# A written table of slots for the loop's tasks, and the gate's narrow products in turn with two runs of values

## The chip, the cores and the metric

One core of one Trainium2 chip runs the whole kernel as one launch. The metric is the device time in microseconds (us) of that launch; for the kernel before, three runs are shown and their median is the number that counts. Four compute engines matter here: TensorE (PE in the profile; its weight loads are PEld), VectorE (DVE), ScalarE (ACT) and GpSimd (POOL). SyncE (SP) only issues DMAs.

## The reference

One layer over 1024 tokens of width 256, in float32: a layer norm, then an attention and a mixture of experts on the same normed rows, both added to the input.

```python
q, k, v = heads(xn @ Wq.T), heads(xn @ Wk.T), heads(xn @ Wv.T)      # 16 heads of 16
scores = einsum('bhid,bhjd->bhij', q, k) / sqrt(16)
std_out = out_proj(softmax(where(mask, scores, neg)))
...
gsa_scores = scores + position_sensitivity * splat_attn              # 8 splats a head
gsa_out = out_proj(softmax(where(mask, gsa_scores, neg)))
attn = (1 - blend) * std_out + blend * gsa_out

logits = xn @ gate_w.T                                               # 16 experts
scores = sqrt(softplus(logits));  top 2 of scores + gate_b
out = einsum('eci,edi->ecd', silu(buf @ W1) * (buf @ W3), W2)        # 128 slots an expert
y = weighted sum of the two experts' rows + shared expert
return x + attn + y
```

So there are two softmaxes for each of the 16 heads over a causal 1024 x 1024 matrix, and beside them 16 routed experts of 128 slots and one shared expert for all 1024 tokens.

## The kernel before

**Prologue.** TensorE's tasks are listed in `PRO`: transposes of the normed rows (`xnT`), projections of the first half of q and k (`proj`), the splats' parameters (`par`), splat features of the first half (`feat`), the gate's logits (`gate`, L736), the values (`v`, four runs, L751), then the second half's projections (`proj1`, L702). Task n of the list goes to PSUM bank n % 5 and waits until the task five before it has been emptied. The gate is 16 products of 128 x 128 weights with 16 columns, each two float32 instructions (32 on the trace); one `v` run is 4 products of 256 columns (8 instructions). The first two `v` runs stand right behind the gate; then TensorE takes the first maxima of group 0 (L770, L775), with the last two `v` runs between them. These maxima need q and k, which SP brings into `stage` (L348).

**Loop.** Eight groups of two heads (g = 0 to 7); in each, six pairs of key blocks (p = 0 to 5), and in each pair four turns, so 24 slots a group. A pair does on TensorE: `pv` of the pair before (L897, 16 instructions), slot 0, `splat` for s = 0 (L879), slot 1, `splat` for s = 1, slot 2, `std` of the next pair for s = 0 (L867, and L870 on the diagonal), slot 3, `std` for s = 1. ScalarE does one exponential (L670) a turn, and then what the slot has for it. VectorE has no work of the attention's own but the copies of the accumulator: `evac` (L1281) before slot 0 (of the group before) and before slot 8. TensorE's first `pv` of the next accumulation waits for that copy.

**Slots.** `PLAN[g][n]` lists the tasks of slot n. Each engine walks the same list in order and takes its own share:
- `max`, `max2` (TensorE L775, L770; VectorE L1215, L1183): row maxima for the next group's softmax shift, 14 tasks a group. In group 0 eight more `pre` maxima of group 0 itself. The last of each half leads to a chain of small VectorE operations, and `shift` (L778, L1229) turns the result; SP then writes it into `qs` (L369).
- `xT`, `gu`, `hT`, `y` of an expert (L801, L813, L817, L822), `sgu`, `shT`, `sy` of a part of the shared one; `weights` and `y` let SP load weights (L520, L521). GpSimd gathers an expert's rows (L452).
- `route` 0 to 7, `rest`, `third`, `product`, `add`: VectorE only (but for two products of `route`); `square`, `p0`, `p1`: ScalarE only; `feat1`: four feature products of the second half (L712) with a ScalarE evacuation (L588).
- `oT`, `oTh`, `rows`, `out`: the output side (L826, L830, L839, L852).

Tasks that need PSUM share three banks (5 to 7) in the order of the table: the task three before has to be emptied first. So TensorE, which runs strictly in order, stops at such a task when VectorE or ScalarE is behind.

**How the slots are given.** Helpers place families of tasks: `spread_late` puts maxima on slots that are no multiple of 4, two a slot; `chain` repeats an expert's steps every 12 slots; `spread` and the list `HALF` place the rest. They are the same for groups 1 to 6.

Of the kernel before, what the change touches and what calls it, by code (L numbers as in the profile page):

```python
# [6 lines left out]
def bass_splat_attention_moe_layer(nc, x, wqkvo, params, w13, w2, ws13, ws2, out):  # L7
# [3 lines left out]
    T, D = x.shape  # L11
# [32 lines left out]
    with ctx:  # L44
# [147 lines left out]
        PRO += [("feat", (tc, w)) for tc in range(NC) for w in range(2)] + [("gate", 0)] + [("v", n) for n in range(NT // 2)]  # L192
# [38 lines left out]
        def slotted(*lists):  # L231
            slots = [[] for _ in range(NSLOT)]
            for entries in lists:
                for at, t in entries:
                    slots[at].append(t)
            return slots

        ROUTE = 8
        CUM, IDS = 4, 7

        def spread_late(tasks, first, last):
            late_slots = [n for n in range(first, last + 1) if n % 4]
            return [(late_slots[len(late_slots) * n // len(tasks)], t) for n, t in enumerate(tasks)]

        def spread(tasks, first, last):
            return [(first + (last + 1 - first) * n // len(tasks), t) for n, t in enumerate(tasks)]

        def chain(steps, count, at, period):  # L250

            return [(at + period * (n // 2) + slot, (kind, n)) for n in range(count) for kind, slot in steps[n % 2]]
        SHARED = ((("sgu", 2), ("shT", 5), ("sy", 6)), (("sgu", 7), ("shT", 9), ("sy", 10)))
        EXPERT = ((("xT", 0), ("gu", 2), ("hT", 5), ("y", 6)), (("xT", 5), ("gu", 7), ("hT", 9), ("y", 10)))

        maxima = spread_late(max0, 0, 6) + [(9, ("shift", 0))] + spread_late(max1, 7, 20) + [(22, ("shift", 1))]
        LATER = 8
        first_rest = [(n // 2, ("pre", t)) for n, t in enumerate(max1[LATER:])] + [(4, ("pre", ("shift", 1)))]
        first_maxima = spread_late(max0, 5, 9) + [(12, ("shift", 0))] + spread_late(max1, 10, 20) + [(22, ("shift", 1))]

        HALF = [(2, ("square", 0)), (3, ("square", 1)),
                (4, ("feat1", (0, 1))), (5, ("feat1", (1, 1))), (6, ("feat1", (0, 0))), (7, ("feat1", (1, 0))),
                (8, ("p0", 4)), (9, ("p0", 5)), (24, ("rest", 4)), (26, ("rest", 5)), (28, ("p1", 4)), (30, ("p1", 5)),
                (34, ("third", 4)), (37, ("third", 5)), (42, ("product", 1)), (44, ("p0", 6)), (46, ("p0", 7)),
                (48, ("rest", 6)), (50, ("rest", 7)), (52, ("p1", 6)), (55, ("p1", 7)), (58, ("third", 6)), (62, ("third", 7))]
        LAST_FEAT = ("feat1", (1, 0))
        S_ROUTE, S_SHARED, S_EXPERT, S_ADD = (8, 31), (32, 148), 56, 156
        OWN_AT = (0, 3)  # L270
        long = HALF + spread([("route", k) for k in range(ROUTE)], *S_ROUTE)

        for half in range(2):
            long += [(at, (kind, n + half * NT // 2)) for at, (kind, n) in chain(SHARED, NT // 2, S_SHARED[half], 12)]
        long += [(S_EXPERT - 24 + 5 * e, ("weights", e)) for e in range(WB - 1)]
        long += chain(EXPERT, E, S_EXPERT, 12)
        long += spread([("add", (k, n)) for n in range(NT) for k in range(2)], S_ADD, 7 * NSLOT + 16)
        AT = {t: at for at, t in long}
        PLAN = []
        for g in range(NG):  # L280
            lists = [[(11, ("oT", 0))], [(at - g * NSLOT, t) for at, t in long if at // NSLOT == g]]
            if g:
                lists.append([(3, ("oT", 1))])
            else:
                lists.append(first_rest)
            if g < NG - 1:
                lists.append(maxima if g else first_maxima)
            if g == NG // 2:
                lists.append([(14, ("rows", (0, 0))), (18, ("rows", (0, 1)))])
            if g == NG - 1:  # L290
                lists.append([(6, ("out", (TC, 0))), (10, ("out", (TC + 2, 0))), (13, ("rows", (1, 0))),
                              (16, ("out", (0, 2))), (19, ("out", (2, 2))), (21, ("oTh", 0))])
            PLAN.append(slotted(*lists))

# [401 lines left out]
        def _(pe):  # L696
# [18 lines left out]
            def prologue(n):  # L715
# [15 lines left out]
                elif kind == "gate":  # L731
                    pe.wait_ge(par_in, 16)
                    pe.wait_ge(pro_act, KD * NC)
                    for t in range(NT):
                        for k in range(KD):
                            last = M(b[:, t * E:(t + 1) * E], xnT[:, k, t * P:(t + 1) * P], gw_sb[:, k, :],  # L736
                                     start=k == 0, stop=k == KD - 1)
# [9 lines left out]
                else:  # L747
                    pe.wait_ge(wvo_in, 32)
                    for i in range(2):
                        for k in range(KD):  # L750
                            last = M(b[:, i * D:(i + 1) * D], xnT[:, k, (2 * a + i) * P:(2 * a + i + 1) * P],  # L751
                                     wt[:, 2, k, :], start=k == 0, stop=k == KD - 1)
# [657 lines left out]
```

## Time and profile before

| | us |
|---|---|
| median of three runs | 357.77 |
| lowest, highest | 357.11, 359.34 |
| the profiled execution, its own time | 356.44 |
| its span, first to last instruction | 354.7 |

| engine | busy us of the span | share |
|---|---|---|
| TensorE | 316.1 | 89% |
| VectorE | 235.8 | 66% |
| ScalarE | 201.4 | 57% |
| GpSimd | 39.7 | 11% |

The span leaves 1.7 us of the execution's time outside. The loop's first `std` starts at 52.2 us and the loop's last `pv` at 345.7 us. TensorE's matmuls are pipelined, so a busy TensorE in a row of the profile can hide short stalls; the granted clock is 1.00 for 2.4 GHz and 0.50 for 1.2 GHz.

### The profile page before, as it was taken

The numbers are of one execution on the slowest core, as the hardware profiler recorded it, in microseconds if no ns is written. First come the engines' busy times: TensorE is split into PE (matmuls) and PEld (weight loads), VectorE is DVE, ScalarE is ACT, GpSimd is POOL, SyncE is SP. The second block draws the span as 40 slices with busy tenths as digits, with TensorE's granted clock in tenths as the row PEclk, the third lists the DMA queues.
The fourth block names the chain that finished last, engine by engine and source line by source line (L and its number), as shares of the span: only waits on it lengthen the run. The fifth ranks groups of instructions, "written<-read, shape, count | busy, mean of one in ns | idle before, by whom it ended". The sixth has DMA issues, their size and how long they took to land.

```text
span 354.7 us, 6091 instructions
## 1 busy us (share of the span) xinstructions
PE 316.1 (89%) x2064; PEld 161.2 (45%) x2064; DVE 235.8 (66%) x735; ACT 201.4 (57%) x300; POOL 39.7 (11%) x59
## 2 busy tenths in 40 slices
PE   0899898977779999999999999999999999999984
PEld 0548533223423455444544455445445554445352
DVE  4858776499997568964766567665766568666424
ACT  1696277575645576654565465555555545647730
POOL 7300000000020000111111111102110004444000
PEclk9998998999978999999999999999999999999999
DMA  7424353224146303635455536554554443222011
GB/s 243 132 43 65 57 99 88 55 43 67 30 65 167 73 2 48 137 112 138 112 140 116 161 87 146 129 143 100 128 145 134 102 80 78 59 72 60 7 59 59
DMA packets 25790, 33.54 MB, mean 95 GB/s; under 512 B 4636, under 2 KB 18556, under 8 KB 25756
## 3 DMA queue, kind: packets, MB, share of 16 engines
q1 hardware_dynamic: 24056, 28.85, 35.3%
q0 software_dynamic: 1536, 4.20, 4.3%
q8 instruction: 18, 0.29, 0.3%
q14 instruction: 16, 0.13, 0.1%
q10 hardware_dynamic: 164, 0.07, 0.1%
HBM read 16.15 MB, written 4.26 MB: 58 GB/s over the span
## 4 chain that ended last, share of the span: by engine, by line
PE 44%; DVE 5%; ACT 2%; issue 2%; DMA 1%; SPq 1%; DVEq 0%
PE ps L897 12%; PE ps L813 6%; PE ps L822 5%; PE ps L879 5%; PE ps L867 4%; PE ps L775 4%; PE ps L852 2%; DMA stage<-split 1%; PE ps L817 1%; PE ps L870 1%; ACT arena_p L670 1%; DVE mx L1215 1%; ACT small L682 1%; PE ps L826 1%; PE ps L801 1%
## 5 line engine op out<-in xcount | busy, mean ns | idle before, releaser
L670 ACT ACTIVATE arena_p<-ps 128x1024 f32<-128x1024 f32 (+1 forms) x192 | 148.0, 808 | 49.6 <-PE ps L879 29.2
L897 PE MATMUL ps<-arena_p,v_full 128*32 128x512 f32 (+3 forms) x768 | 72.6, 496 | 0.0
L1183 DVE CUSTOM_DVE_ANT_0 ps<-ps,mask_r 128x128 f32<-128x128 f32 (+3 forms) x128 | 61.7, 501 | 11.6 <-PE ps L775 6.9
L775 PE MATMUL ps<-stage 96*128 96x512 bf16 (+3 forms) x160 | 50.6, 354 | 8.1 <-DVE mx L1215 3.7
L867 PE MATMUL ps<-stage 98*128 98x512 bf16 (+1 forms) x192 | 51.6, 333 | 3.7 <-ACT arena_p L670 3.0
L1215 DVE TENSOR_REDUCE mx<-ps 128x1 f32<-128x512 f32 x64 | 43.9, 686 | 14.5 <-PE ps L775 14.1
L879 PE MATMUL ps<-stage 98*128 98x512 bf16 (+1 forms) x192 | 47.2, 334 | 2.5 <-ACT arena_p L670 2.3
L452 POOL DMA_INDIRECT wt<-xn_scratch,ids_sb x16 | 15.3, 954 | 235.3 <-PE ps L801 107.6
L897 PEld LDWEIGHTS ps<-arena_p,v_full 128*32 128x32 f32 x768 | 20.1, 110 | 34.6 <-issue 30.0
L775 PEld LDWEIGHTS ps<-stage 96*128 96x128 bf16 x160 | 15.6, 99 | 29.6 <-issue 22.2
L675 ACT ACTIVATE small<-ps 128x176 f32<-128x176 f32 x24 | 7.6, 317 | 37.2 <-PE ps L813 37.2
L879 PEld LDWEIGHTS ps<-stage 98*128 98x128 bf16 x192 | 15.6, 99 | 28.8 <-ACT arena_p L670 13.1
L867 PEld LDWEIGHTS ps<-stage 98*128 98x128 bf16 x192 | 18.6, 99 | 19.5 <-ACT arena_p L670 5.8
L1237 DVE SCALAR_TENSOR_TENSOR small<-small,ps 128x176 f32<-128x176 f32 x24 | 8.1, 338 | 29.0 <-ACT small L675 12.7
L822 PE MATMUL ps<-arena_o,small 88*128 88x256 f32 x96 | 25.7, 389 | 1.9 <-ACT small L682 1.8
L870 PE MATMUL ps<-mask_t,ident_b 128*128 128x128 bf16 x128 | 25.9, 221 | 0.0
L682 ACT ACTIVATE small<-ps 88x256 f32<-88x256 f32 x24 | 9.1, 379 | 29.3 <-PE ps L817 28.0
L813 PE MATMUL ps<-w_sb,wt 128*128 128x352 f32 x64 | 22.3, 471 | 1.2 <-DVE wt L1231 0.9
L822 PEld LDWEIGHTS ps<-arena_o,small 88*128 88x128 f32 x96 | 16.9, 189 | 8.3 <-issue 5.5
L477 POOL DMA_INDIRECT split<-ye_scratch,gidx x16 | 15.4, 962 | 45.9 <-DMA ye_scratch<-wt 28.8
L1005 DVE TENSOR_TENSOR acc<-ps,acc 128x256 f32<-128x256 f32 (+1 forms) x14 | 7.5, 538 | 16.2 <-PE ps L852 11.3
L1183 DVE DVE_READ_ACCUMULATOR2_ANT mx<- 128x1 f32 x128 | 18.1, 142 | 0.0
(199 smaller groups left out, 374.2 us busy)
## 6 DMA issues: line engine op xcount, KB each, us to landing
w_sb<-in_w_dram SPq DMA_DIRECT2D x16, 352.0 KB
stage<-split SPq DMA_DIRECT2D x48, 96.0 KB
stage<-split SPq DMA_DIRECT2D x96, 32.0 KB
stage<-split SPq DMA_DIRECT2D x48, 64.0 KB
arena_o<-in_w_dram SPq DMA_DIRECT2D x16, 176.0 KB
ye_scratch<-wt SPq DMA_DIRECT2D x16, 128.0 KB, 2.6
stage<-split SPq DMA_DIRECT2D x32, 48.0 KB
acc<-in_x_dram SPq DMA_DIRECT2D x2, 512.0 KB, 4.7
```

Of the source, the lines that this page charges most:

```text
L452: nc.gpsimd.indirect_dma_start(out=xe[:, e % XB, :], out_offset=None, in_=xn_d[:, :], in_offset=bass.IndirectOffsetOnAxis(ap=ids_sb[:, e:e ...
L477: nc.gpsimd.indirect_dma_start(out=gath[:, k, n, :], out_offset=None, in_=ye_d[:, :], in_offset=bass.IndirectOffsetOnAxis(ap=gidx[:, k, n: ...
L670: A(to, ps[:, 1 + 2 * s:3 + 2 * s, off:CH], ACT.Exp, scale=SCALE).then_inc(done, 1)
L775: ins = M(b[:, 0:n1 - n0], qs[0:KR, pr, h, it * P:(it + 1) * P], ks[0:KR, pr, h, n0:n1], start=True, stop=True)
L813: ins = M(b[:, 0:2 * I], lhs, w13_sb[:, wb, k, :], start=k == 0, stop=k == KD - 1)
L822: ins = M(b[:, 0:D], hT[:, c, :], w2_sb[:, wb, c, :], start=c == 0, stop=c == 1)
L867: ins = M(b[:, off:CH], ks[:, pr, h, (jb + s) * P:(jb + s + 1) * P], qs[:, pr, h, ic * CH + off:(ic + 1) * CH], start=True, stop=not diag)
L870: ins = M(b[:, off:off + P], ident_b[:, :], mask_t[:, :], start=False, stop=True)
L879: ins = M(ps[:, 1 + 2 * s + h, off:CH], fk[:, pr, h, (jb + s) * P:(jb + s + 1) * P], fq[:, pr, h, ic * CH + off:(ic + 1) * CH], start=Fals ...
L897: ins = M(ps[c:c + 2 * HD, 0, off:CH], v_full[:, jb + s, g * GH + h, :], of, start=jb + s == 0, stop=end or last, skip_group_check=last an ...
L1183: return V.tensor_tensor_reduce(row, row, mask_r[:, CH - row.shape[1]:CH], 1.0, NEG, ALU.add, ALU.max, to)
L1215: V.reduce_max(to, b[:, 0:n1 - n0], AX.X).then_inc(aux_free, 1)
```

## The change

Two edits.

**The table.** The helpers and lists that made `PLAN` are gone, and all 8 x 24 slots are written out. Same tasks, same three banks, same engines; what differs is the slot, and the order within a slot. `AT` is read back from the table. The task that starts SP's load of the shared weights, the loads of q, k and features and so on still hang on the same tasks and slots.

**The prologue.** `("v", 0)` now stands before `("gate", 0)` in `PRO`, and the three tasks `v 0`, `gate`, `v 1` are issued by one function: two tokens' blocks of the gate (8 instructions), one block of values (4 instructions), four times over. It waits at its start for all three banks, for the values' weights, for the parameters and for all of `xnT`.

```diff
-        PRO += [("feat", (tc, w)) for tc in range(NC) for w in range(2)] + [("gate", 0)] + [("v", n) for n in range(NT // 2)]
+        PRO += [("feat", (tc, w)) for tc in range(NC) for w in range(2)] + [("v", 0), ("gate", 0), ("v", 1), ("v", 2), ("v", 3)]
...
-        maxima = spread_late(max0, 0, 6) + [(9, ("shift", 0))] + spread_late(max1, 7, 20) + [(22, ("shift", 1))]
...
+        PLAN = [
+            [
+                [("pre", ("max", (1, 4, 0))), ("pre", ("max", (1, 4, 1))), ("pre", ("max", (1, 5, 0))),
+                 ("pre", ("max", (1, 5, 1)))],
+                [("pre", ("max", (1, 6, 0))), ("pre", ("max", (1, 6, 1))), ("pre", ("max", (1, 7, 0)))],
+                [("pre", ("max", (1, 7, 1)))],
+                [("max2", (0,))],
+                [("square", 0), ("square", 1), ("pre", ("shift", 1))],
+                [("max2", (1,)), ("p0", 4), ("max", (0, 2, 0))],
+                [("feat1", (0, 1)), ("feat1", (1, 1)), ("max", (0, 3, 0))],
+                [("max", (1, 2, 0))],
+                [("max", (1, 3, 0)), ("route", 0)],
+                [("p0", 5)],
+                [("max", (0, 4, 0)), ("feat1", (0, 0)), ("feat1", (1, 0)), ("max", (0, 4, 1)), ("max", (0, 5, 0)),
+                 ("max", (0, 5, 1))],
+                [("route", 1), ("oT", 0)],
+                [("shift", 0), ("max", (0, 6, 0))],
+                [("max", (0, 6, 1)), ("max", (0, 7, 0)), ("max", (0, 7, 1)), ("max", (1, 4, 0))],
+                [("max", (1, 4, 1)), ("route", 2), ("route", 3)],
...
+                [("route", 5), ("rest", 5)],
+            ],
...
-                elif kind == "gate":
-                    pe.wait_ge(par_in, 16)
-                    pe.wait_ge(pro_act, KD * NC)
-                    for t in range(NT):
-                        for k in range(KD):
-                            last = M(b[:, t * E:(t + 1) * E], xnT[:, k, t * P:(t + 1) * P], gw_sb[:, k, :],
-                                     start=k == 0, stop=k == KD - 1)
...
+            def gate_and_values():
+
+                n = PRO.index(("gate", 0))
+                for at in (n - 1, n, n + 1):
+                    pe.wait_ge(*emptied[at - PB])
+                pe.wait_ge(wvo_in, 32)
+                pe.wait_ge(par_in, 16)
+                pe.wait_ge(pro_act, KD * NC)
+                gates, runs = ps[:, n % PB, :], (ps[:, (n - 1) % PB, :], ps[:, (n + 1) % PB, :])
+                for half in range(NT // 2):
+                    for t in (2 * half, 2 * half + 1):
                         for k in range(KD):
...
+                            scores = M(gates[:, t * E:(t + 1) * E], xnT[:, k, t * P:(t + 1) * P], gw_sb[:, k, :],
+                                       start=k == 0, stop=k == KD - 1)
+                    if half == NT // 2 - 1:
+                        scores.then_inc(pro_full, 1)
+                    last = values(half, half % 2, runs[half // 2])
+                    if half % 2:
+                        last.then_inc(pro_full, 1)
```

The slots that the prediction speaks of, before and after (read from both tables; "3:5" is slot 5 of group 3; `m h it pc` is a `max` of head h, row block it, key half pc):

| task | before | after |
|---|---|---|
| `pre` maxima of group 0 | 2 in each of 0:0 to 0:3 | 4 in 0:0, 3 in 0:1, 1 in 0:2 |
| `square` 0, 1 | 0:2, 0:3 | both 0:4 |
| `feat1` (0,1), (1,1) | 0:4, 0:5 | both 0:6 |
| `feat1` (0,0), (1,0) | 0:6, 0:7 | both 0:10 |
| `max2` 0 and 1 of group 0 | 0:5, 0:5 | 0:3, 0:5 |
| `p0` 4, 5 | 0:8, 0:9 | 0:5, 0:9 |
| `m 1 3 0`, `route` 0 | 0:9, 0:8 | 0:8, 0:8 |
| `route` 1, 2, 3 | 0:11, 0:14, 0:17 | 0:11, 0:14, 0:14 |
| `rest` 4, 5 | 1:0, 1:2 | 0:19, 0:23 |
| `route` 5, 6, 7 | 0:23, 1:2, 1:5 | 0:23, 1:1, 1:6 |
| `max2` 0, 1 in group 3 | both 3:1 | 3:2, 3:3 |
| `hT` 3, `y` 3 | 3:5, 3:6 | 3:4, 3:6 |
| `shift` 0, `xT` 4, `gu` 4 | 3:9, 3:8, 3:10 | 3:8, 3:9, 3:11 |
| `m 0 6 1`, `m 0 7 0`, `m 0 7 1` | 3:11, 3:11, 3:13 | 3:11, 3:12, 3:12 |
| `xT` 6, `gu` 6 | 3:20, 3:22 | 3:18, 3:22 |
| maxima in 6:5 | 1 (and 1 in 6:6, 2 in 6:7) | 5 (none in 6:6, 6:7) |
| `out` (0,2), (2,2) | 7:16, 7:19 | 7:18, 7:19 |
| `oTh` 0 | 7:21 | 7:23 |

No slot before has more than two maxima. After, ten slots have three or more (0:0, 0:1, 0:10, 0:13, 0:17, 1:18, 5:1, 5:9, 6:5, 6:10). `hT`, `y` and `xT` of the other experts stay or move by one or two slots.

## Rows read from the trace of the kernel before

**Rows 1.** The page: span, and busy time of each engine.
```profile
span 354.7 us, 6091 instructions
PE 316.1 (89%) x2064; PEld 161.2 (45%) x2064; DVE 235.8 (66%) x735; ACT 201.4 (57%) x300; POOL 39.7 (11%) x59
```

**Rows 2.** Busy by stretch: length, PE, PEld, DVE, ACT, POOL, granted clock, DMA, GB/s.
```profile
27.44:30.97 3.53, 3.53 (x34) 3.53 (x32) 3.20 (x4) 2.97 (x4) 0.00 (x0) 1.00 0.33 57
30.97:34.38 3.41, 3.41 (x10) 2.78 (x11) 3.31 (x3) 1.93 (x2) 0.00 (x0) 0.50 0.60 84
...
52.17:54.86 2.69, 1.65 (x12) 0.85 (x13) 0.95 (x3) 2.68 (x4) 0.00 (x0) 1.00 0.87 190
54.86:58.28 3.42, 3.42 (x13) 1.64 (x12) 2.17 (x5) 3.12 (x5) 0.00 (x0) 0.50 0.36 82
58.28:69.21 10.93, 10.69 (x63) 3.25 (x61) 4.87 (x21) 5.21 (x10) 0.00 (x0) 1.00 0.22 35
69.21:102.65 33.44, 25.37 (x215) 10.68 (x214) 30.99 (x107) 21.64 (x27) 0.00 (x0) 1.00 0.29 52
102.65:105.93 3.28, 2.75 (x7) 0.92 (x7) 3.11 (x14) 1.41 (x2) 1.84 (x2) 0.50 0.52 78
105.93:109.48 3.55, 3.55 (x23) 1.24 (x23) 1.42 (x5) 2.05 (x2) 0.21 (x1) 0.50 0.73 218
...
175.25:211.55 36.30, 34.91 (x245) 18.28 (x243) 23.04 (x76) 20.41 (x33) 3.78 (x4) 1.00 0.52 134
...
321.72:354.70 32.98, 26.47 (x190) 13.19 (x188) 14.44 (x36) 14.15 (x20) 2.81 (x3) 1.00 0.15 48
```

**Rows 3.** Who TensorE waited for, 69.3 to 106 us: total, times, longest.
```profile
PE ps L775 <- DVE mx L1215: 2.0, 2, 1.7
...
PE ps L784 <- DVE mx L1183: 1.8, 1, 1.8
...
PE ps L826 <- DVE mx L1183: 1.0, 1, 1.0
```

**Rows 4.** Timeline of TensorE in the prologue: start, length, instructions, idle before.
```profile
27.44 3.82 PE L736 MATMUL ps<-prm,xx 128*128 128x16 f32 x32
31.10 5.31 PE L751 MATMUL ps<-wt,xx 128*128 128x256 f32 x16
36.25 0.50 PE L770 MATMUL ps<-stage 96*128 96x128 bf16 x4
...
36.75 1.89 PE L751 MATMUL ps<-wt,xx 128*128 128x256 f32 x8
38.48 0.54 PE L775 MATMUL ps<-stage 96*128 96x512 bf16 x2
...
42.52 0.22 PE L778 MATMUL ps<-ident_b,mhl 128*16 128x128 bf16 x1 [1.55 <-DVE mhl L1005]
```

**Rows 5.** Timeline of SyncE's queue, 18 to 42 us: the loads of q and k.
```profile
19.68 11.72 SPq L348 DMA_DIRECT2D stage<-split  x12
```

**Rows 6.** The page's DMA issues: count, KB each, us from issue to landing.
```profile
ye_scratch<-wt SPq DMA_DIRECT2D x16, 128.0 KB, 2.6
```

**Rows 7.** Who VectorE waited for, 52 to 58.9 us.
```profile
DVE mx L1215 <- PE ps L775: 4.3, 3, 2.7
```

**Rows 8.** Who VectorE waited for, 58.9 to 69.3 us.
```profile
DVE ps L1183 <- PE ps L775: 3.3, 2, 2.0
```

**Rows 9.** Timeline of TensorE: a feature product of two steps, and what follows.
```profile
63.85 1.08 PE L712 MATMUL ps<-xx,small 128*64 128x512 f32 x4 [0.24 <-ACT rest L588]
...
65.72 0.34 PE L775 MATMUL ps<-stage 96*128 96x384 bf16 x1
```

**Rows 10.** Timeline of VectorE: the first and the last end of route 0.
```profile
70.74 0.28 DVE L1005 TENSOR_TENSOR g_last<-w_sb,prm 128x128 f32<-128x128 f32 x1
...
72.68 0.70 DVE L1183 CUSTOM_DVE_ANT_0 ps<-ps,mask_r 128x512 f32<-128x512 f32 x1
```

**Rows 11.** Who TensorE waited for in group 3, 175.25 to 211.55 us (six such rows).
```profile
PE ps L822 <- ACT small L682: 0.3, 1, 0.3
```

More of the change, by code:

```diff
@@ L229, in bass_splat_attention_moe_layer @@
         max1 = [("max", (h, it, pc)) for h in range(GH) for it in range(TC, NT) for pc in range(2)]
[L231 to L236, printed above, removed]
         ROUTE = 8
         CUM, IDS = 4, 7
-        def spread_late(tasks, first, last):
-            late_slots = [n for n in range(first, last + 1) if n % 4]
-            return [(late_slots[len(late_slots) * n // len(tasks)], t) for n, t in enumerate(tasks)]
@@ L247, in spread @@
[L247 to L254, printed above, removed]
@@ L256, in bass_splat_attention_moe_layer @@
-        maxima = spread_late(max0, 0, 6) + [(9, ("shift", 0))] + spread_late(max1, 7, 20) + [(22, ("shift", 1))]
-        LATER = 8
[L258 to L267, printed above, removed]
+        LATER = 8
@@ L268, in bass_splat_attention_moe_layer @@
         LAST_FEAT = ("feat1", (1, 0))
-        S_ROUTE, S_SHARED, S_EXPERT, S_ADD = (8, 31), (32, 148), 56, 156
         OWN_AT = (0, 3)
[L271 to L277, printed above, removed]
@@ L295, in bass_splat_attention_moe_layer @@
+        AT = {t: g * NSLOT + n for g, slots in enumerate(PLAN) for n, tasks in enumerate(slots) for t in tasks
+              if t[0] not in ("max2", "max", "shift", "pre", "oT")}
         END = [("rowsh", 0), ("oTh", 1), ("out", (TC, 1)), ("rowsh", 1), ("out", (TC + 2, 1))]
@@ L749, in prologue, with values @@
                     for i in range(2):
-                        for k in range(KD):
-                            last = M(b[:, i * D:(i + 1) * D], xnT[:, k, (2 * a + i) * P:(2 * a + i + 1) * P],
-                                     wt[:, 2, k, :], start=k == 0, stop=k == KD - 1)
-                last.then_inc(pro_full, 1)
+                        last = values(2 * a + i, i, b)
+                last.then_inc(pro_full, 1)
+            def values(t, i, b):
+                for k in range(KD):
+                    last = M(b[:, i * D:(i + 1) * D], xnT[:, k, t * P:(t + 1) * P], wt[:, 2, k, :], start=k == 0, stop=k == KD - 1)
+                return last
+            def gate_and_values():
[8 more added lines that the diff above has]
+                    for t in (2 * half, 2 * half + 1):
+                        for k in range(KD):
+                            scores = M(gates[:, t * E:(t + 1) * E], xnT[:, k, t * P:(t + 1) * P], gw_sb[:, k, :],
[4 more added lines that the diff above has]
+                    if half % 2:
+                        last.then_inc(pro_full, 1)
             def weights_of(kind, a):
@@ L929, in _ @@
             n_v, n_p = PRO.index(("v", 0)), PRO.index(("proj1", (0, 0)))
-            for n in range(n_v + 2):
+            for n in range(n_v):
                 prologue(n)
+            gate_and_values()
             pe.wait_ge(wide_ready, 1)
@@ L941, in _ @@
                 if n in (AB, 2 * AB - 1):
-                    prologue(n_v + 2 + n // 4)
+                    prologue(n_v + 3 + n // 4)
                 aux(-1, t, 0)
```

208 lines of the change are left out of this document (192 added, 16 removed).

## The prediction

> **What bounds the kernel now.** I read the page first: TensorE is busy 316.1 of 354.7 us [rows 1]. That says "TensorE", and for most of the loop it is right, but a share of the span hides where it is not. So I cut the span into stretches [rows 2]. In a steady group (the fourth, 36.30 us) TensorE is busy 34.91 us, so 1.39 us is all that a better order can take off there, save for drains too short for the profile. VectorE has 23.04 us of work in it. The stretch 69.21 to 105.93 us (most of group 0 and the start of group 1) is another matter: VectorE is busy 30.99 + 3.11 = 34.10 of 36.72 us, TensorE only 25.37 + 2.75 = 28.12, so TensorE idles 8.60 us. The waits name the cause: TensorE stood 2.0 + 1.8 + 1.0 us for VectorE's maxima to empty a bank [rows 3]; the routing runs on VectorE between them. VectorE bounds this stretch. And right ahead of it, 52.17 to 69.21 us, VectorE is busy only 0.95 + 2.17 + 4.87 = 7.99 of 17.04 us: the engine that bounds the next 37 us had idled for 9.05.
>
> The third thing is the granted clock. It is 1.00 nearly everywhere and 0.50 in three stretches [rows 2]: 30.97 to 34.38, 54.86 to 58.28, and 102.65 to 109.48 us. Before the second and third TensorE had gaps; before the first it had none (busy 3.53 of 3.53 us), but all it did was the gate's narrow products.
>
> **The change, part by part.**
>
> *Gate and values.* The 32 narrow instructions took 31.10 - 27.44 = 3.66 us at clock 1.00; the 16 instructions of two value runs behind them took 36.25 - 31.10 = 5.15 us, mostly at 0.50; at 1.00, eight take 38.48 - 36.75 = 1.73 us, so sixteen 3.46 [rows 4]. Same instructions after the change, so at full clock the block takes 3.66 + 3.46 = 7.12 us where it took 8.81: 1.69 us less, if the clock holds. It should: no long run of narrow products is left, each eight (0.9 us) is followed by 0.87 us of 256-column ones. Does the gain travel on? Next is the first maximum, which needs q and k. SP issued the last of these loads at 19.68 + 11.72 = 31.40 us [rows 5]; with the 2.6 us that a larger transfer takes to land [rows 6] that is 34.0, about when TensorE would now come (34.6). VectorE had finished its splitting work about then too, and idled until the first maximum. What comes next, up to the loop's first `std`, is a chain through TensorE and VectorE (1.55 us wait at 42.52 us, [rows 4]) and shifts as a whole. The block's new wait at its start is for three banks at once, those of the second parameter task and of the first two features, which VectorE and ScalarE empty before the last features that TensorE computes ahead of the block; the gate's reader (VectorE, behind the first maxima) comes long after the block. I take -1.6, with bounds 0 (clock falls all the same, or q and k late) and -1.7.
>
> The Trainium skill ("TensorE: Matmul & The Clock Gate", section "HAM oscillation — how this bites in real kernels") lays a fallen clock to gaps in which TensorE idles. By that rule the interleaving would bring nothing here, since the block has no gap before or after; the sum would be 1.6 us smaller. The row at 27.44 us, no idle and a fall at its end, speaks against the rule being all there is, and I go by the row; what it would mean is a rival below.
>
> *Groups 0 and 1.* VectorE's work is conserved, so the end of its bound stretch moves by as much of its earlier idling as the table removes. Two places. First, slot 0:0 now has four maxima, 0:1 three: of the three waits for a maximum (4.3 us, longest 2.7) the longest stands before the loop's first product and stays, the other 1.6 go, less about 0.2 [rows 7]. Second, the features. A product of two steps takes TensorE 65.72 - 63.85 = 1.87 us [rows 9], two of them 3.7 us, in which VectorE gets nothing: it waited 3.3 us for two maxima behind these [rows 8]. Now both stand in 0:10, where VectorE has in hand `m 1 3 0` and `m 0 4 0` (0.6 each, a 512-column one takes 0.70) and `route` 0 (72.68 - 70.74 = 1.94 us) [rows 10]: 3.2 of the 3.7 us are covered. Together 1.4 + 3.2 = 4.6 us. TensorE can follow, as it idles 8.60 us in the stretch. Against it: `square` 0 and 1 both in 0:4 hold ScalarE for two microseconds ahead of an exponential, but `pv` covers most of it; `rest` 4, 5 (1.2 us each) now stand before the group's end, ahead of `evac`, so the first `pv` of group 1 waits for VectorE, where before the waits stood a little later. It is the same debt, paid elsewhere. SP: the shared weights' load hangs on the last feature, now 0:10; the feature loads of slots 0:7 and 0:8 no longer queue behind it, the q and k loads of 0:10 on still do; their readers come 20 us later. I take -4.6, bounds 0 and -8.6.
>
> *The loop's clock.* The low stretches of the loop, 3.42 and 6.83 us long, cost at most half: 1.7 and 3.4 us. Where gaps will fall next I can't say; the worst TensorE waits shrink, but a new one stands at the end of group 0. I take 0, bounds -3.4 and +3.4.
>
> *Steady groups 2 to 5.* Six waits of 0.2 to 0.3 us a group, such as `y` on ScalarE's copy [rows 11]. `hT` 3 is a slot further from `y` 3, `xT` 6 four slots ahead of `gu` 6 instead of two, `max2` no longer right behind `hT` and `xT`, `m 0 7 0` not right behind `gu` and `oT`. That aims at all six. Some come back in other places, so I take 0.6 of 1.39 us, four times: -2.4. Bounds: -5.6, and +2.8 if one 512-column maximum (0.70 us, [rows 10]) a group is waited for anew. SP's order is nearly that of before: `y` moves by a slot at most, and the last q and k loads are needed a slot later in group 3. The gathers on GpSimd have an expert's step to spare.
>
> *Groups 6 and 7.* Five maxima in 6:5 with three banks: VectorE frees one every 0.6 us, so TensorE waits about 1 us there, and saves the small waits behind; 0. In the last stretch TensorE idles 6.5 of 32.98 us [rows 2], mostly in the dependent ending. The output products now stand after both `splat`s of their pair and `oTh` after the last, so that ScalarE's exponential and VectorE's copy are covered: -0.4, bounds -1 and +1.
>
> Sum: -1.6 - 4.6 + 0 - 2.4 + 0 - 0.4 = -9.0 us. The profiled execution took 356.44 us (span 354.7), so 347.4; the median of the runs shown is 1.33 above it, so 348.8.
>
> **Rivals.** About 1% (3.6 us) is what a measurement of this kernel can tell from no change.
>
> (a) The clock falls in the prologue all the same, or was never the narrow products' doing: all but the first term, 350.4. For it, the rule above; against it, the row. 0.12.
>
> (b) The lead of VectorE is lost at the seam of groups 0 and 1: `route` 5, `rest` 5, `evac` and `route` 6 stand in one row on VectorE, over 7 us, and TensorE behind them waits so long that it pays 3 us of idling and 1.7 us of low clock. Then 353.5. For it: TensorE would reach group 1 well ahead of VectorE. Against: the debt stands before, too. 0.13.
>
> (c) Slower: the bunches. Ten slots have three or more maxima on three banks; the old table spread them two by two. Each maximum past the banks costs TensorE 0.6 us if VectorE is not idle when the bunch comes, and it is busy 23.04 of 36.30 us even in a steady group. At 1.5 us a bunch that is +15, against -9: 364. The point from which it decides is 1.3 us a bunch (+12.6, past +1%). Against it: slots behind a bunch are left empty, and in group 0 VectorE wants the work. 0.08.
>
> (d) The stalls only move: TensorE is the bound at 89% and its work is unchanged, gains of 2 us or less, 356. 0.07.
>
> The forecast itself, 344.5 to 352.5, has 0.60.
>
> **How the numbers follow.** Faster by over 1% (under 354.2): 0.60 + 0.12 + most of (b), 0.08: 0.80. Same: the rest of (b), and (d): 0.12. Slower: (c), 0.08. The range from 344.0 to 355.5 takes in (a) and (b) and leaves (c), (d) and a larger gain (the clock's -3.4) out: about 0.2.
>
> **What would show it.** Prologue: the rows of the block (L736 and L751 now mixed) in 7.1 us, and granted clock 1.00 from 27 to 37 us; the loop's first L867 at 50.5 instead of 52.17. Group 0: VectorE idle between first L867 and the 9th us of features down from 9.05 to about 4.5 us; the L897 run that opened at 105.93 (second of group 1) at about 99 to 100. Steady groups 35.7 us instead of 36.30. The forecast is wrong if that L897 run stands after 103, if a steady group grows, or if waits of TensorE on L1215 or L1183 behind the bunches sum to over 5 us.

## The result and the profile after

| | before | after |
|---|---|---|
| median of the runs measured side by side | 358.29 us (4 runs) | 342.33 us (4 runs) |
| range of these runs | 357.11 to 359.34 | 340.96 to 344.22 |
| profiled execution | 356.44 us | 344.22 us |
| its span | 354.7 us | 342.4 us |

The changed kernel is faster: ratio 0.956, 95% interval 0.950 to 0.962, some 16 us. The forecast was 348.8 us with a range down to 344.0, so the sign was right and the size wrong, beyond the lower end. The two profiles are 12.2 us apart; the profile of after happens to be the slowest of its four executions, that of before is below its median, and the 3.7 us between the two differences are taken up further down.

The page of the kernel after, its span and its engines, to be held against [rows 1]:

```profile
span 342.4 us, 6091 instructions
PE 309.8 (90%) x2064; PEld 159.4 (47%) x2064; DVE 236.4 (69%) x735; ACT 201.1 (59%) x300; POOL 39.6 (12%) x59
```

The instructions are the same in number. PE's busy time is 6.3 us lower, since some of it was time at the lower clock and some was waiting that its records don't show as such; the other 6.0 us of the shorter span are idle time that is gone. Busy time by stretch of the kernel after (length, PE, PEld, DVE, ACT, POOL, granted clock, DMA, GB/s), for [rows 2]: the block of gate and values; two stretches from the loop's first `std` to the second `pv` of group 1; groups 2 to 6 whole.

```profile
29.11:36.25 7.14, 7.14 (x51) 6.63 (x50) 6.51 (x6) 5.38 (x6) 0.00 (x0) 1.00 0.46 69
52.16:68.68 16.52, 14.66 (x98) 5.71 (x100) 11.21 (x41) 14.34 (x19) 0.00 (x0) 1.00 0.42 81
68.68:101.01 32.33, 26.88 (x209) 11.25 (x205) 29.89 (x104) 19.65 (x26) 0.65 (x1) 0.96 0.33 55
...
132.09:166.44 34.35, 34.11 (x244) 17.99 (x242) 25.12 (x75) 21.82 (x34) 3.78 (x4) 1.00 0.48 117
166.44:201.43 34.99, 34.73 (x245) 18.22 (x244) 23.70 (x79) 20.47 (x33) 3.78 (x4) 1.00 0.57 139
201.43:236.39 34.96, 34.83 (x251) 18.99 (x249) 25.31 (x80) 19.89 (x32) 3.78 (x4) 1.00 0.57 142
236.39:272.70 36.31, 35.05 (x244) 17.98 (x242) 22.14 (x72) 20.86 (x34) 1.89 (x2) 1.00 0.49 124
272.70:310.46 37.76, 35.38 (x238) 17.47 (x236) 23.08 (x70) 20.48 (x34) 13.23 (x14) 1.00 0.29 71
```

The block is 7.14 us long at clock 1.00, where it was 8.81. In groups 2 to 4 PE idles 0.24, 0.26 and 0.13 us; before, group 3 alone had 1.39 [rows 2]. The only wait of TensorE left in group 3 (engine, tile, line, whom it waited for: us in total, times, longest) stands where there were six [rows 11]:

```profile
PE ps L1042 <- ACT arena_p L829: 0.2, 1, 0.2
```

Here is the whole difference between the two profiles. The marks are the starts of instructions in the timelines; a group runs from its first `pv` to that of the next group.

| stretch | before | after | difference | forecast |
|---|---|---|---|---|
| start to the block of gate and values | 27.44 | 29.11 | +1.67 | none |
| the block, to the first maximum | 8.81 | 7.14 | -1.67 | -1.6 |
| to the loop's first `std` | 15.92 | 15.91 | 0.0 | 0 |
| to the start of group 2 | 86.08 | 79.93 | -6.15 | -4.6 |
| groups 2 to 5 | 147.56 | 140.61 | -6.95 | -2.4 |
| group 6 | 35.91 | 37.75 | +1.84 | 0 |
| group 7, to its last `pv` | 24.00 | 22.89 | -1.11 | -0.4 (with the ending) |
| ending | 8.98 | 9.10 | +0.1 | |
| sum | 354.70 | 342.44 | -12.2 | -9.0 |

### The profile page after: what moved, and what is told of

The parts are those of the page before. It is cut to its first block, busy times and chain, and to the rows that moved or that the text cites. A ratio compares the mean times of both kernels' runs of the same rounds, so it can differ in the third digit from the quotient of the medians.

```text
span 342.4 us, 6091 instructions
## 1 busy us (share of the span) xinstructions
PE 309.8 (90%) x2064; PEld 159.4 (47%) x2064; DVE 236.4 (69%) x735; ACT 201.1 (59%) x300; POOL 39.6 (12%) x59
## 4 chain that ended last, share of the span: by engine, by line
PE 73%; SPq 9%; DVE 9%; ACT 4%; issue 2%; DMA 2%; DVEq 0%
PE ps L1072 19%; PE ps L1042 9%; PE ps L988 9%; PE ps L1054 8%; PE ps L997 7%; PE ps L950 7%; SPq L507 4%; SPq L522 3%; PE ps L861 2%; PE ps L1027 2%; ACT arena_p L829 2%; PE ps L1001 2%; SPq L519 2%; DVE ps L1359 2%; PE ps L871 2%
## 5 line engine op out<-in xcount | busy, mean ns | idle before, releaser
L1042 PE MATMUL ps<-stage 98*128 98x512 bf16 (+1 forms) x192 | 50.9, 330 | 5.7 <-ACT arena_p L829 3.4
L950 PE MATMUL ps<-stage 96*128 96x512 bf16 (+3 forms) x160 | 49.3, 344 | 5.8 <-DVE mx L1359 3.5
L1054 PE MATMUL ps<-stage 98*128 98x512 bf16 (+1 forms) x192 | 45.4, 326 | 0.1
L1457 DVE COPY pv_sb<-ps 128x512 f32<-128x512 f32 x15 | 10.4, 691 | 10.0 <-PE ps L1072 9.9
```

The lines of the kernel that those rows point to most:

```text
L950: ins = M(b[:, 0:n1 - n0], qs[0:KR, pr, h, it * P:(it + 1) * P], ks[0:KR, pr, h, n0:n1], start=True, stop=True)
L1042: ins = M(b[:, off:CH], ks[:, pr, h, (jb + s) * P:(jb + s + 1) * P], qs[:, pr, h, ic * CH + off:(ic + 1) * CH], start=True, stop=not diag)
L1054: ins = M(ps[:, 1 + 2 * s + h, off:CH], fk[:, pr, h, (jb + s) * P:(jb + s + 1) * P], fq[:, pr, h, ic * CH + off:(ic + 1) * CH], start=Fals ...
```

## The experiments

The new table writes out every group, so each part of the change can be put into the old kernel, or taken out of the new one, alone. "Old slots" are those that the expressions removed by the diff give, written out as a table. All ratios are to the kernel before, measured on the same chip in turn with it. "Low" is a stretch at granted clock 0.50. A task is written as in the prediction; `m` is a maximum.

### The prologue alone, the table alone

**e1_prologue**: old slots, new order of gate and values.

```
-  PRO += [...] + [("gate", 0)] + [("v", n) for n in range(NT // 2)]
+  PRO += [...] + [("v", 0), ("gate", 0), ("v", 1), ("v", 2), ("v", 3)]
```

> The prologue's edit alone, on the table of before. Theory A (narrow products brought the clock down): the block of gate and values takes 7.1 us at granted clock 1.00 instead of 8.8 us, and the first maximum follows at once; 1.7 us faster than before in a profile with an equal start, ratio about 0.995, no other stage changed. Rival (the fall belongs to the moment, not to the products): a low stretch still falls on or right behind the block in the profile, and the ratio is 1.000.

Measured: ratio 0.996 (0.992 to 1.000; 10 runs against 11), so that the total alone can't be told from no change; the stage shows it. In its profile the block is 7.13 us long at clock 1.00, and the first `std` comes 23.04 us after the block's start, where it came 24.73 after: 1.69 us less, the forecast's number. The groups are as before (38.66, 40.67, 37.21, 36.30, 37.95, 36.30, 35.92, 24.00). The block in the busy time by stretch:

```profile
28.55:35.68 7.13, 7.13 (x51) 6.63 (x50) 6.50 (x6) 5.38 (x6) 0.00 (x0) 1.00 0.45 69
```

**e2_table**: new table, old prologue (the diff's `PRO` line undone).

> The written table alone, on the prologue of before. Theory: it carries nearly all, about 12 to 14 of the 16 us between the medians, ratio 0.960 to 0.966; the block of gate and values keeps its 8.8 us with clock 0.50 behind the narrow products. Rival (the two edits need each other, the earlier start of the maxima being what feeds VectorE): ratio 0.975 or more.

Measured: ratio 0.960 (0.953 to 0.967). Block 8.81 us, low from 30.6 to 34.0. So nearly all of the gain is the table's, 14.4 us between the medians (342.97 against 357.35). From the first `std` to the second `pv` of group 1 (the distance that the prediction speaks of: 53.76 us before) it takes 46.76, to group 2 77.77 where before took 86.08.

### Which groups

**e3_groups01**: before, with the new slots in groups 0 and 1. **e4_groups2345**: before, with the new slots in groups 2 to 5.

```
-  PLAN = [ <old slots of groups 0 to 7> ]
+  PLAN = [ <new slots of groups 0, 1>, <old slots of groups 2 to 7> ]      # e3
+  PLAN = [ <old slots of groups 0, 1>, <new of 2 to 5>, <old of 6, 7> ]    # e4
```

> The new slots of groups 0 and 1 only; groups 2 to 7 and the prologue as before. Theory (VectorE's early idling is filled): from the loop's first std to the second pv of group 1, 48.8 us instead of 53.8, and about 6 us off up to the start of group 2's second pair; groups 2 to 5 stay at 36.3 to 38.0 us each. Ratio 0.980 to 0.985. Rival (the lead of the first groups is what shortened groups 2 to 5 too, by loads and gathers that come earlier): groups 2 to 5 shorten by 1 us or more each, ratio under 0.975.

Measured: ratio 0.974 (0.967 to 0.981), profile 348.49 us. The place is right and the size larger than expected. The second `pv` of group 1 stands 46.77 us after the first `std`, as with the whole table; from group 2 on nothing moves (36.90, 36.30, 37.95, 36.30, 36.13, 24.00).

> The new slots of groups 2 to 5 only; all else as before. Theory (the small waits and the pipeline's drains behind each were the gain): groups 2, 3, 4 take 34.4, 35.0, 35.0 us instead of 37.0, 36.3, 38.0, and group 5 stays at 36.3; 7 us less in all, ratio 0.980. Rival (as in the prediction: waits mostly come back elsewhere): 2.4 us less, ratio 0.993.

Measured: ratio 0.982 (0.975 to 0.989), profile 350.18 us, 6.3 below that of before. Groups 0 and 1 take what they took (38.66 and 40.72), groups 2 to 5 take 34.36, 35.00, 34.95 and 36.85. The steady groups of e4, in the busy time by stretch:

```profile
138.16:172.52 34.36, 34.12 (x244) 17.99 (x242) 24.87 (x74) 21.58 (x34) 3.79 (x4) 1.00 0.49 117
172.52:207.52 35.00, 34.73 (x247) 18.26 (x245) 23.70 (x79) 20.48 (x33) 3.79 (x4) 1.00 0.56 138
```

Profile to profile, e3 gives 7.95 and e4 6.26 us, 14.2 together, and the whole table (e2) 14.1: the two add up, and groups 6 and 7 add about nothing.

**e6_no67**: after, with the old slots in groups 6 and 7.

> The changed kernel, with the slots of before in groups 6 and 7. Theory (the bunch of five maxima in 6:5 and a step of an expert that waits behind it cost more than the new order of group 7 saves): group 6 takes 35.9 to 36.1 us instead of 37.75, group 7's part up to its last pv 24.0 instead of 22.9; 0.5 to 0.8 us faster than the changed kernel, ratio to before 0.954. Rival (group 6 is longer for a reason of the groups before it, not of its slots): group 6 stays at 37.8 and the ratio goes up to 0.960.

Measured: ratio 0.955 (0.950 to 0.959), median 341.84 us. Group 6 goes back from 37.75 to 35.92 and group 7 from 22.89 to 24.00, group 5, whose last tasks belong with these, from 36.31 to 36.86: 0.2 us of net gain, nothing that a measurement can tell. The new slots of groups 6 and 7 bring nothing that shows.

### Groups 0 and 1: which step

**e10_feats_back**: the new table (old prologue, as e2), with the features' squares and products back in the slots that they had.

```
-  0:4 square 0, square 1   0:6 feat1 (0,1), feat1 (1,1)   0:10 feat1 (0,0), feat1 (1,0)
+  0:2 square 0   0:3 square 1   0:4 feat1 (0,1)   0:5 feat1 (1,1)   0:6 feat1 (0,0)   0:7 feat1 (1,0)
```

> The written table on the prologue of before, with the two squares and the four feature products of group 0 back in slots 0:2 to 0:7. Theory (VectorE's debt: it starves while TensorE makes features, and what it starves the bound stretch ends later by): from the loop's first std to the first pv of group 1, 3 to 4 us more than the 40.9 us of the table alone. Rival (the maxima's other moves carry the gain): under 1 us more.

Measured: 346.77 us, and the first `pv` of group 1 stands 44.34 us after the first `std`, where e2 has 40.85: 3.5 us, for a forecast of 3.2. Whom VectorE waited for while the features are made, e2 (57.3 to 71 us) and then e10 (58 to 70 us):

```profile
DVE ps L1362 <- PE ps L954: 1.9, 2, 1.3
...
DVE pv_sb L1460 <- PE ps L1076: 0.9, 1, 0.9
...
DVE ps L1362 <- PE ps L949: 0.3, 1, 0.3
```

```profile
DVE ps L1362 <- PE ps L954: 3.3, 2, 1.8
DVE mT L1408 <- PE ps L957: 1.9, 1, 1.9
DVE ps L1362 <- PE ps L949: 1.4, 1, 1.4
DVE pv_sb L1460 <- PE ps L1076: 0.6, 1, 0.6
```

In these stretches VectorE waits 7.2 us for TensorE in e10 and 3.1 in e2; all rows but that of `pv_sb` are maxima and the shift, which TensorE reaches only after features. Over the distance from the first `std` to the second `pv` of group 1 (50.53 and 46.76 us) VectorE is busy 40.12 and 40.18 us: the same work, 3.8 us more of idling. This is the starvation that the prediction priced, shown by itself. It is one execution of each, but e2, e3 and e11, all with the features in their new slots, are within 0.2 us over this distance (46.76, 46.77 and 46.95).

**e11_rest_back**: e2 with `rest` 4 and 5 back in group 1.

```
-  0:19 rest 4   0:23 rest 5
+  1:0 rest 4    1:2 rest 5
```

> The written table on the prologue of before, with rest 4 and rest 5 back in slots 1:0 and 1:2. Theory (VectorE's work up to the routing's end is the same in either order): TensorE's 1.9 us wait early in group 1 gets shorter but a wait of the same size comes by the products of routing step 7; the second pv of group 1 starts within 0.5 us of where it does with the table alone, counted from the first std (46.8 us). Rival: it starts a microsecond or more earlier, and the new places of rest 4 and 5 were a loss.

Measured: 343.04 us, 46.95 us to the second `pv` of group 1 against 46.76. The two tasks (1.2 us each on VectorE) may stand on either side of the seam: the debt stays the same, as forecast. The waits fell otherwise than expected: of the 1.9 us for a maximum early in group 1, 1.1 is left, and the rest is not a wait by the products of `route` 7 but 1.0 us in two waits of a `std` for ScalarE's exponential.

### The steady groups: which half

**e8_experts**: before, with only the experts' tasks (`xT`, `gu`, `hT`, `y`, and the shared ones) of groups 2 to 5 in their new slots. **e9_maxima**: before, with only the maxima, shifts and transposes of the output there. In group 3, for instance:

```
   old:  3:1 hT 2, xT 3, max2 0, max2 1  3:5 hT 3, m 1 2 0   3:11 oT 0, m 0 6 1, m 0 7 0   3:20 xT 6
   e8:   3:4 hT 3                        3:5 m 1 2 0         3:11 gu 4, oT 0, m 0 6 1, m 0 7 0   3:18 ..., xT 6
   e9:   3:1 hT 2, xT 3, oT 1   3:2 y 2, max2 0   3:3 gu 3, max2 1, m 0 2 0   3:11 oT 0, m 0 6 1   3:12 m 0 7 0, ...
```

> The kernel before, with only the experts' tasks (xT, gu, hT, y and the shared ones) of groups 2 to 5 in their new slots; maxima, shifts and output tasks stay. Theory (half of the waits are y behind hT and gu behind xT, half are maxima behind a bank): group 3 takes 35.6 to 35.8 us instead of 36.30 (35.00 with all moved), waits of L822's and L813's place gone, those of the maxima left. Rival (the moves only work together): 36.1 to 36.5.

Measured: 360.19 us in one execution, and group 3 takes 36.51 us, where it took 36.30: the rival's value, not the theory's. Five waits are left, one of them longer than any of before. Group 3 of e8 in the timeline of TensorE (start, length, instructions, idle before and whose work ended it):

```profile
187.98 0.60 PE L1005 MATMUL ps<-ident,pv_sb 128*128 128x128 f32 x4
188.41 0.33 PE L954 MATMUL ps<-stage 96*128 96x384 bf16 x1
189.44 0.38 PE L954 MATMUL ps<-stage 96*128 96x512 bf16 x1 [0.70 <-DVE small L1417]
```

The second maximum behind `gu` 4 and `oT` 0 needs the bank in which `gu` 4's result still lies. In the old table `gu` 4 stood a slot earlier, in the new one `m 0 7 0` stands a slot later; with one of the two moved alone, they meet.

> The kernel before, with only the maxima, shifts and output tasks of groups 2 to 5 in their new slots; the experts' tasks stay. Theory: group 3 takes 35.5 to 35.7 us instead of 36.30, the waits of L822 and L813 left, those of L775 and L770 gone; the gains of this kernel and of the one with the experts moved add up to 1.3 us in group 3. Rival: 36.1 to 36.5.

Measured: 357.36 us in one execution, group 3 35.78 us, and two waits in it:

```profile
PE ps L1005 <- DVE small L1417: 0.4, 1, 0.4
PE ps L954 <- DVE mx L1362: 0.3, 1, 0.3
```

That is just above the theory's 35.5 to 35.7, but the waits that were to be left (L822 and L813 of before) are gone, and an `oT` behind a `gu` and one maximum wait instead. So in group 3 the experts' half costs 0.2 us, the other half brings 0.5, and both together 1.3. Over groups 2 to 5 the experts' half brings 0.4 us (147.19 for 147.56), the other half 1.0 (146.57), and both (e4) 6.4. They are not terms of a sum. All of these tasks take their banks from the same three, in the order in which they stand, so what a task waits for depends on which three stand ahead of it. Groups 0 and 1 of these two executions (41.45, 40.77 and 40.30, 40.82 us) differ from before without an edit there; they come back below, under the clock.

### The write that queues, and the best version

**e7_sp_late**: after, with SyncE's feature loads for group 1 begun at slot 0:5 instead of 0:0.

```
-  for j in range(2 * at, min(2 * at + 2, N_F)):
+  first = at if g else at - 5
+  for j in range(max(2 * first, 0), max(min(2 * first + 2, N_F), 0)):
```

The reason for it is a row of after. Whom TensorE waited for, 57 to 66 us, and SyncE's queue around that time:

```profile
PE ps L1042 <- DMA stage<-mT: 1.3, 1, 1.3
```

```profile
55.38 2.89 SPq L522 DMA_DIRECT2D stage<-split  x4
58.31 1.40 SPq L519 DMA_DIRECT2D stage<-split  x2
59.76 1.39 SPq L522 DMA_DIRECT2D stage<-split  x2
61.19 1.35 SPq L528 DMA_DIRECT2D stage<-mT  x2
```

The `std` at 63.60 us needs the shifts that the write at 61.19 puts into `stage`. The eight feature loads ahead of it hold the queue from 55.38 to 61.19, at about 0.7 us each. VectorE had turned the shift at 59.48 us (its copy into `mT`, 59.27 to 59.48), so the queue held the write back by 1.7 us.

> The changed kernel, in which SyncE issues group 1's feature loads from slot 0:5 on instead of 0:0 on, so that the write of group 0's second shift (slot 0:4) does not queue behind eight of them. Theory (the 1.3 us for which the std at 63.6 us waited for that write is SyncE's queue, which the prologue's edit does not bring forward): the write is issued as soon as VectorE has turned the shift, the wait is gone whatever the start of the execution, ratio to before 0.953, 1 us faster than the changed kernel. Rival (the wait is the write's own travel time): no change, and the wait of 1.3 us stands in the profile.

Measured: ratio 0.953 (0.950 to 0.957), median 341.43 us (6 runs), 0.9 below after's, with overlapping intervals. In its profile the write is issued at 58.28 us, the feature loads behind it, the wait is gone, and group 0 takes 35.17 us where after has 36.41:

```profile
58.28 1.43 SPq L525 DMA_DIRECT2D stage<-mT  x2
59.75 2.88 SPq L519 DMA_DIRECT2D stage<-split  x4
```

Group 1 stays as long as in after (38.31 and 38.20 us). That the wait is the queue's is shown; a gain of 1 us in the total fits and is not clear of noise.

**e13_best**: e7 with the old slots in groups 6 and 7 (e6).

> The changed kernel with both edits together: groups 6 and 7 in the slots of before, and group 1's feature loads from slot 0:5 on. If both theories hold their gains add up: ratio to before 0.949 to 0.952, 1.5 to 2 us faster than the changed kernel. If neither does, 0.956.

Measured: ratio 0.953 (0.949 to 0.957), median 341.59 us (341.27 to 342.08, 6 runs). That is 0.7 us below after and not the 1.5 to 2 expected of it. Its profiled execution, 341.27 us, is the shortest of the profiled ones, but by the runs neither this nor e7 can be told from after.

### What brings the clock down

**e12_gate_last**: before, with the gate's 32 narrow instructions behind two runs of values.

```
-  PRO += [...] + [("gate", 0)] + [("v", n) for n in range(NT // 2)]
+  PRO += [...] + [("v", 0), ("v", 1), ("gate", 0), ("v", 2), ("v", 3)]
```

> The kernel before, with the gate's block of 32 narrow instructions behind the first two runs of values instead of ahead of them. Theory (it is the narrow products that bring the clock down): the values run at clock 1.00, the granted clock falls to 0.50 at or right behind the gate's block, and the first maxima and values behind it run at half speed. Rival (it falls at this point of the prologue whatever runs): the clock falls at 30 to 31 us, while the values are computed, as with the kernel before.

Measured: 357.67 us in one execution. The prologue of e12, timeline of TensorE, and its stretches in the busy time:

```profile
28.34 3.72 PE L911 MATMUL ps<-wt,xx 128*128 128x256 f32 x16
31.89 3.64 PE L892 MATMUL ps<-prm,xx 128*128 128x16 f32 x32
35.38 0.49 PE L949 MATMUL ps<-stage 96*128 96x128 bf16 x4
...
35.87 3.29 PE L911 MATMUL ps<-wt,xx 128*128 128x256 f32 x8
```

```profile
28.34:31.89 3.55, 3.55 (x18) 3.14 (x17) 3.21 (x4) 2.99 (x4) 0.00 (x0) 1.00 0.30 51
31.89:35.40 3.51, 3.51 (x34) 3.50 (x33) 3.29 (x3) 2.88 (x4) 0.00 (x0) 1.00 0.61 88
36.20:39.60 3.40, 3.40 (x10) 2.31 (x9) 1.43 (x8) 0.40 (x1) 0.00 (x0) 0.50 0.35 54
```

The fall has moved with the gate. It comes at 36.20, 4.3 us after the narrow run began, and now costs the second pair of value runs (3.29 us for eight instructions, 1.73 at full clock [rows 4]). TensorE had no idle ahead of it. The total does not show it: one execution, within the range of before.

## Why the prediction was right or wrong

The forecast's largest miss is the steady groups (6.95 us for 2.4); the sections go through the terms in the order of time.

**The prologue: right.** The block takes 7.14 us for a forecast of 7.12, and the 1.6 to 1.7 us travel to the first `std`, in after and, alone, in e1. In the nine profiles in which the 32 narrow products stand in one block (before, e2, e3, e4, e8 to e12), the clock fell 3.3 to 4.6 us after that block began, in e12 later than in the others as the block stood later; in the five in which eight of them take turns with four wide ones (after, e1, e6, e7, e13) it did not. Rival (a) is out. The fall in before and in e12 follows on a run with no idle (busy 3.53 of 3.53 [rows 2], 3.51 of 3.51 us), and it moves when the narrow run is moved. By the Trainium skill ("TensorE: Matmul & The Clock Gate", section "HAM oscillation — how this bites in real kernels") a fallen clock goes back to gaps in which TensorE idles. The traces here do not agree for this fall. What it is in the narrow products that does it was not taken apart. In the profile of after the gain can't be seen in the total, because that execution began 1.67 us late: the block began at 29.11 instead of 27.44. Its first instruction of TensorE stands at 10.66 us (10.07 in before), and the first record of full clock at 16.68 us (13.90 in before); the 512-column projections take 1.06 us up to there and 0.59 from there on. This start-up differs from execution to execution of kernels with the same prologue (13.5 to 16.0 us over the profiles with the old one).

**Groups 0 and 1: the mechanism right, two terms missing.** VectorE does bound the stretch, and what its end gains is what its idling loses. From the first `std` to the second `pv` of group 1, before takes 53.76 us with VectorE busy 42.09, so idle 11.67; e2 takes 46.76 with 40.18 busy, so idle 6.58. The idling falls by 5.1, for 4.6 forecast. e10 shows the features' part alone (3.5 for 3.2), and of the three waits for a maximum ahead of the first `pv` of group 0 [rows 7] e2 has only the longest left (2.7 us), as forecast. In after the first 16.52 us from that `std` leave VectorE 5.31 us idle, where about 4.5 was the sign to look for. The missing terms:

- *Work moved behind the bound stretch.* The other 1.9 of the 7.0 us is VectorE's work itself: 42.09 against 40.18 us ahead of that `pv`. I took VectorE's work there as conserved, and it is not. Between the first and the second `pv` of group 1 the old table gives VectorE 8.00 us of work, the new one 5.63; the difference is done later, where TensorE is the bound and VectorE has time (24.23 of 31.01 us busy). Not all of this is the table's: e12, with the old table but no low clock in group 1, has 6.88 us there and 40.88 up to that `pv`. So about 1.2 of the 1.9 us goes with the low clock of group 1, under which VectorE does more ahead of that `pv`, and 0.7 with the table. Which tasks carry these was not taken apart, except that `rest` 4 and 5 don't (e11).

```profile
97.52:105.93 8.41, 5.79 (x46) 2.14 (x44) 8.00 (x31) 3.33 (x5) 1.84 (x2) 0.80 0.42 64
```

```profile
92.82:98.73 5.91, 5.86 (x49) 2.39 (x48) 5.63 (x23) 2.80 (x5) 0.00 (x0) 0.78 0.35 59
```

  These are that stretch in before and in e2.

- *The clock of the loop.* I took 0. Before has 6.8 us of low clock in group 1 [rows 2]; each of the new table's profiles has one stretch of 3.4 us at the seam or in group 1. What such a stretch costs depends on who is the bound. e12's group 1 has none and takes 38.60 us. With 6.8 us of it and the same slots, group 1 takes 40.74 us in before and 40.67 to 40.82 in e1, e4, e8 and e9, however long group 0 was before it. So 6.8 us cost 2.1, less than half, as VectorE bounds the first of it. (This is in part the same time as the 1.2 us above, seen from TensorE.) With the new table, 3.4 us of low clock that begin within a us of group 1's start (e2, e3, e6, e10, e11) go with a group 1 of 36.9 to 37.5 us; the same 3.4 us begun 4.7 to 5.3 us into it (after, e7, e13) go with 38.2 to 38.3, about a us more. That the place makes the difference is not shown by a run of its own.

A loss that I had argued away goes against these: the `std` at 63.6 us that waits 1.3 us for a write in SyncE's queue. The prediction looked at that queue only for its loads, and found their readers 20 us later; the write of the shifts in the same queue has a reader 2 us later. With the prologue quicker by 1.7 us and group 0 quicker too, TensorE reaches it before SyncE has worked off its list, which in after has no pause from 46.04 us to the write. e1, e2 and e3, with one part alone, don't wait; after and e6 do (1.3 us each). So two parts of the change, each a gain, meet here in a wait that neither has alone, and e7 takes it out. Net of its start, 1.67 us late, the second `pv` of group 1 stands at 99.3 us, inside the forecast's "99 to 100": by a larger gain and two losses, not for the reason given.

**Rival (b), the seam.** Its wait exists: TensorE stands 1.88 us for VectorE at the end of group 0 and 1.18 us at the start of group 1, together the 3 us that the rival named. The timeline of TensorE in after:

```profile
91.25 0.22 PE L1045 MATMUL ps<-mask_t,ident_b 128*128 128x128 bf16 x1
93.35 0.38 PE L950 MATMUL ps<-stage 96*128 96x512 bf16 x1 [1.88 <-DVE mx L1359]
...
97.27 0.38 PE L950 MATMUL ps<-stage 96*128 96x512 bf16 x1 [1.18 <-DVE mx L1359]
```

It is the rest of VectorE's debt, smaller than before's [rows 3], and did not eat the gain.

**The steady groups: the term that was mis-sized.** This is the step that failed. Groups 2 to 5 gave 6.95 us (e4 alone: 6.40), for 2.4 forecast and a bound of 5.6. Two errors add. First, I let 0.6 of 1.39 us a group go, "some come back in other places"; in groups 2 to 4 none did (1.88, 1.39 and 1.77 us of idling before, 0.24, 0.26 and 0.13 after), while group 5 stayed at 36.31. Second, the bound was wrong in kind: it was the idle time that the profile shows, and a stall costs more than that. The row at 91.25 above shows it: a 128-column product has a record of 0.22 us, but the next product starts 0.06 later (91.08, 91.14 in the same timeline). When a wait follows, its last 0.16 us are lost as well, yet count as busy: the product at 93.35 started 1.88 us after that record's end and 2.04 after the time at which it could have. The same holds for the 512-column products (0.38 us long, 0.22 apart). With six or seven waits a group, that is up to a us a group on top of the idle time, which the prediction had only as "drains too short for the profile". In group 2 it fits: idling 1.64 less, six waits less at 0.16 are 0.96, together 2.6, for 2.65 measured. Groups 3 and 4 (1.31 and 2.99 less) are not so clean one by one; a maximum has crossed from the one's side to the other's. Over the three, the idling is 4.4 less and the views list 18 waits less, 2.9 at 0.16: 7.3 us, for 6.95 measured. The 0.16 is an estimate from the starts and lengths of these rows; no run varied it alone.

**Groups 6 and 7, and rival (c), the bunches.** Group 6 grew by 1.84 us and group 7 shrank by 1.11, where 0 and -0.4 stood. Behind the five maxima of slot 6:5 TensorE waited little; the timeline of after there:

```profile
276.87 1.08 PE L950 MATMUL ps<-stage 96*128 96x512 bf16 x3
278.25 0.73 PE L950 MATMUL ps<-stage 96*128 96x512 bf16 x2 [0.29 <-DVE mx L1359]
...
282.69 1.13 PE L997 MATMUL ps<-arena_o,small 88*128 88x256 f32 x4 [0.69 <-DVE mT L1405]
```

That is 0.3 us where rival (c) needed 1.3 a bunch. Over the whole of after TensorE's maxima wait 4.2 us for VectorE's, 3.1 of them at the seam; the sign for (c) was over 5 us behind the bunches. Part of group 6's length is work: PE is busy 35.38 us in it, before 34.09, while it is busy less in the groups around.

**Between the medians.** The last 3.7 us are differences between executions: the profile of before is 1.9 us below its median, that of after, with its late start, 1.9 above. Of 33 times of before, measured beside the experiments, 23 lie at 355.9 to 358.3 us with a mean granted clock of 0.977 to 0.983, ten at 358.9 to 360.1 with 0.971 to 0.976; the profile shown is one of the first kind (13.7 us low, 0.981), and the four executions of after lie at 0.992 to 0.998. A mean of 0.976 to 0.971 over 358 us is 17 to 21 us at 0.50. Where the further low time may lie, e8, e9 and e12 show: with the old slots in group 0, they have 6.8, 3.4 and 6.8 us of low clock inside it, and it takes 41.45, 40.30 and 41.43 us where the other three profiles with those slots (before, e1, e4) take 38.66. But e9 and e12, which lack other low stretches of before, are as long as the first kind (357.36, with 1.0 us less in groups 2 to 5, and 357.67 us); only e8, with 6.8 us in each of groups 0 and 1, is like the second (360.19 us, 0.975). In the eight profiles with the new slots (or e10's) the loop has no low stretch that begins before the last us of group 0. So the table may also spare the kernel, in some executions, up to 2.8 us in group 0. That this is what makes the ten times longer is likely from the clocks and not shown, and why it falls in some executions only stays open. So does which single moves in the steady groups carry the gain: e8 and e9 only show that it is neither half alone.

## What to carry to other kernels

Where one engine bounds a stretch, what counts is its idling ahead of and inside that stretch, and whether some of its work can wait until another engine is the bound: count both. A wait of TensorE costs its idle time and the overlap with the next product that it lost (by estimate 0.16 us here), so many small waits are worth more than the profile's idle column; and tasks that take turns at the same few banks have to be moved as one order, since half a move can bring a wait that neither order has. When an earlier stage gets quicker, look again at every queue that works through a fixed list, for the one short write behind many loads.

## What the runs showed of the hardware

In nine profiles 32 float32 instructions of 16 columns stood in one run without a gap, at two places of the prologue; in each the granted clock fell to 0.50, 3.3 to 4.6 us after the run's start, and stayed there for 3.4 us. Split into eights with four 256-column instructions between, it did not fall there in any of five. What a stretch at 0.50 cost depended on where it fell: 1.7 us of 3.4 in the prologue (8.81 against 7.14 us), where TensorE had nothing to wait for, 2.8 of 6.8 in group 0, 2.1 of 6.8 in group 1, and 0.5 of 3.4 between the first `std` and the first `pv` (6.69 us in before and e4, which have it there, 6.16 in e1, e8, e9 and e12, which have not and share the slots). SyncE issued its loads at about 0.7 us each: eight of them took 5.8 us, and a write behind them, whose data was ready, stood for 1.7.
